# Attention's first step up to its exponentials, the second's scores and the third's mask tiles inside the last projection batch

## The reference

```
x = x + xattn(layernorm(x), ctx, ctx, mask, bias)     # x, ctx: (8, 512, 512)
x = x + ffn(layernorm(x))

def xattn(Q, K, V, mask, bias):
    q, k, v = heads(Q @ Wq.T + bq), heads(K @ Wk.T + bk), heads(V @ Wv.T + bv)
    scores = einsum('bhqd,bhkd->bhqk', q, k) / sqrt(32)
    scores = where(mask == 0, -1e9, scores) + bias    # bias: (1, 16, 512, 512)
    return merge(softmax(scores) @ v) @ Wo.T + bo
```

## Time and profile before

| what | value |
|---|---|
| median of three runs | 1814.23 us |
| the profiled execution | 1813.97 us, span 1812.1 us |
| TensorE, VectorE, ScalarE, GpSimd busy | 99%, 57%, 45%, 46% of the span |
| project | 0 to about 291 us |
| attend | about 291 to 861 us |
| blend | the rest |

### The profile page before, as it was taken

One profiled execution on the slowest core, in us unless ns is written; L12 is line 12 of the kernel. 1 busy time (PEld: TensorE's weight loads), 2 busy tenths in 40 slices (PEclk: granted clock), 3 DMA queues, 4 the chain that ended last, 5 costly groups with the idle time before them and its releaser, 6 DMA issues.

```text
span 1812.1 us, 29631 instructions
## 1 busy us (share of the span) xinstructions
PE 1786.0 (99%) x10784; PEld 1335.4 (74%) x10784; DVE 1039.6 (57%) x2431; ACT 815.5 (45%) x1814; POOL 833.0 (46%) x371
## 2 busy tenths in 40 slices
PE   8999998999999999999999999999999999999999
PEld 6888885555555555555778888888888888888887
DVE  6565556999999999998842334224332242342411
ACT  4222224999999999998232212113131131311300
POOL 1211127999999999997221231222312322223211
PEclk9999998999999999999999999999999999999999
DMA  8998999445436426330543554535546355464453
GB/s 292 339 359 315 324 335 376 144 140 192 136 121 207 140 95 233 105 119 19 200 131 117 199 179 162 203 123 191 180 140 231 123 187 174 138 210 163 150 187 128
DMA packets 198142, 339.97 MB, mean 188 GB/s; under 512 B 10608, under 2 KB 52208, under 8 KB 197488
## 3 DMA queue, kind: packets, MB, share of 16 engines
q1 hardware_dynamic: 194736, 325.50, 53.1%
q0 software_dynamic: 3264, 12.58, 1.9%
HBM read 268.84 MB, written 69.21 MB: 187 GB/s over the span
## 4 chain that ended last, share of the span: by engine, by line
PE 50%; DVE 1%; ACT 0%; issue 0%; POOL 0%; DVEq 0%
PE n_ps_y L1572 19%; PE n_ps_h L1551 19%; PE n_ps_m L1475 9%; PE n_ps_y L1475 3%; PE n_ps_m L1469 1%; DVE k_x L1318 0%; DVE h_bias L1237 0%; DVE k_x L1173 0%; PE n_ps_y L1469 0%; PE n_ps_h L1524 0%; PE n_ps_h L1527 0%; DVE h_k L1246 0%; DVE n_stats L1176 0%; POOL n_g_l L1145 0%; ACT L1431 0%
## 5 line engine op out<-in xcount | busy, mean ns | idle before, releaser
L1145 POOL TENSOR_TENSOR n_g_l<-h_pos,n_g_h 128x512 fp32r<-128x512 f32 x128 | 175.2, 1369 | 602.8 <-DVE n_g_h L1326 602.8
L1551 PE MATMUL n_ps_h<-n_zT_h,n_w 128*128 128x512 f32 x1024 | 336.7, 390 | 1.4 <-ACT h_pos L1431 1.4
L1572 PE MATMUL n_ps_y<-n_w,n_g_h 128*128 128x512 f32 x1024 | 316.6, 390 | 0.3 <-POOL n_g_l L1145 0.3
L1431 ACT ACTIVATE h_pos<-n_ps_h 128x512 f32<-128x512 f32 x128 | 75.8, 599 | 512.4 <-PE n_ps_h L1551 512.3
L1326 DVE CAST n_g_h<-h_pos 128x512 fp32r<-128x512 f32 x128 | 55.3, 434 | 379.5 <-ACT h_pos L1431 379.5
L1551 PEld LDWEIGHTS n_ps_h<-n_zT_h,n_w 128*128 128x128 f32 x1024 | 192.3, 188 | 41.5 <-issue 1.8
L1572 PEld LDWEIGHTS n_ps_y<-n_w,n_g_h 128*128 128x128 f32 x1024 | 191.2, 188 | 39.7 <-POOL n_g_l L1145 0.7
L1572 PE MATMUL n_ps_y<-n_w,n_g_l 128*128 128x512 f32 x512 | 199.3, 389 | 0.0
L1551 PE MATMUL n_ps_h<-n_zT_l,n_w 128*128 128x512 f32 x512 | 199.2, 389 | 0.0
L932 ACT ACTIVATE l_tiles<-l_tiles,a_nmax 128x512 f32<-128x512 f32 x256 | 182.6, 717 | 13.9 <-DVE a_nmax L873 13.9
L932 ACT ACTIVATE a_t_s<-a_t_s,a_nmax 128x512 f32<-128x512 f32 x256 | 182.8, 718 | 0.0
(11 more groups left out here) (198 smaller groups left out, 3158.2 us busy)
## 6 DMA issues: line engine op xcount, KB each, us to landing
n_w<-wf_d SPq DMA_DIRECT2D x256, 512.0 KB, 4.2
a_pos<-pos_d SPq DMA_DIRECT2D x24, 1024.0 KB, 5.6
l_tiles<-in_x SPq DMA_DIRECT2D x8, 1024.0 KB, 10.1
l_bias<-in_mask SPq DMA_DIRECT2D x8, 1024.0 KB, 14.4
k_d<-p_k_s SPq DMA_DIRECT2D x8, 1024.0 KB, 12.1
pos_d<-p_pos SPq DMA_DIRECT2D x8, 1024.0 KB, 13.4
v_d<-p_v_s SPq DMA_DIRECT2D x32, 256.0 KB, 6.6
wf_d<-p_wf_h SPq DMA_DIRECT2D x16, 512.0 KB, 5.8
```

The source lines that it names most:

```text
L1145: pool.tensor_tensor(out=g_l[:, f % NG, :], in0=g_f[:, f % NG, :], in1=g_h[:, f % NG, :].bitcast(F32), op=ALU.subtract).then_inc(g_low, 1)
L1551: last = pe.matmul(ps_h[:, f % 2, :], stationary, moving, start=i == 0, stop=i == len(passes) - 1)
L1572: last = pe.matmul(ps_y[:, t, :], gs[i], w2[:, f % NW, j, :], start=f == 0 and m == 0, stop=f == NF - 1 and m == 2)
```

## The change

`Late` gets a third pair of buffers, the semaphores of attention's scores, minima and exponentials, the small table of minima and sums, and the four PSUM banks that project used for turning x and attend for its scores. `k_s` and `pos` of project now lie in the third pair. In the last projection batch:

- TensorE makes the four scores of step 0 between the first and the second Q product, and the scores of step 1 after the last Q product;
- VectorE makes the four minima of step 0 between its first and second eviction of Q;
- ScalarE makes the four exponentials of step 0 after its last copy of feed-forward weights;
- GpSimd makes the mask tiles of step 2 in one instruction after its last difference of feed-forward weights;
- SP loads the bias rows of step 3 before it stores V. These rows lie where `pos` was, so SP first waits until the store of `pos` has landed.

Attend leaves these parts out. Nothing that is computed changes.

```diff
@@ class Late
-        self.tiles = [sb("tiles0"), sb("tiles1")]
-        self.bias = [sb("bias1"), sb("bias2")]
+        self.tiles = [sb("tiles0"), sb("tiles1"), sb("tiles2")]
+        self.bias = [sb("bias1"), sb("bias2"), sb("bias3")]
...
@@ project
-        x_raw, xn = late.tiles
-        c_raw, m_raw = late.bias
+        x_raw, xn, k_s = late.tiles
+        c_raw, m_raw, pos = late.bias
...
                 sp.wait_ge(bank_free, NPB + NVQ * b + NT)
+                if not more:
+                    sp.wait_ge(pos_out, 16 * (B + 1))
+                    load_bias(3)
                 for c in range(NC):
                     sp.dma_start(tokens(v_d[B * c + b]), v_s[:, :, c * P:(c + 1) * P]).then_inc(v_out, 16)
...
+            def third_mask_tiles():
+                pool.wait_ge(ahead.bias_in[2], 16)
+                pool.wait_ge(k_out, 16 * (B + 1))
+                pool.tensor_tensor(out=late.tiles[2][:, :, :], in0=ahead.pos[:, 2:3, :].broadcast_to([P, HG, S]),
+                                   in1=late.bias[1][:, :, :], op=ALU.subtract).then_inc(ahead.nbm_pool, HG)
...
+            def first_minima():
+                for i in range(HG):
+                    dve.wait_ge(late.scored, i + 1)
+                    dve.wait_ge(ahead.nbm_pool, HG)
+                    gate(dve, passed)
+                    dve.tensor_tensor_reduce(late.tiles[0][:, i:i + 1, :], late.ps[:, i:i + 1, :],
+                                             late.tiles[0][:, i:i + 1, :], 1.0, 3.0e38, ALU.add, ALU.min,
+                                             late.nmax[:, 0, i:i + 1]).then_inc(late.summed, 1)
...
+                if not more:
+                    for i in range(HG):
+                        act.wait_ge(late.summed, i + 1)
+                        act.activation(late.tiles[0][:, i, :], late.tiles[0][:, i, :], ACT.Exp, scale=-1.0,
+                                       bias=late.nmax[:, 0, i:i + 1], accum_out=late.total[:, 0, 0, i:i + 1]) \
+                            .then_inc(late.exped, 1)
...
                 for c in range(NC):
                     product(Q_AT + c, features((w_h[0], w_l[0]), (xT_h, xT_l), c))
+                    if not more and c == 0:
+                        pe.wait_ge(ahead.qk_in[0], 32)
+                        pe.wait_ge(fac_row_done, B)
+                        scores(0)
+                if not more:
+                    pe.wait_ge(late.summed, HG)
+                    scores(1)
@@ attend
-            sp.dma_start(bias_rows(0, HG, 3), bias[0, 0:HG, 3 * P:4 * P, :].rearrange("h p n -> p h n")) \
-                .then_inc(ahead.bias_in[3], 16)
...
-                        if g or j > 1:
+                        if g or j > 2:
                             step(hg, g, j, half)
...
-                    for i in range(HG):
+                    for i in range(HG if g or j > 1 else 0):
```

More of the change, by code:

```diff
@@ L86, in __init__, with sb @@
     def __init__(self, nc, stack):
-        def sb(name):
-            return stack.enter_context(nc.sbuf_tensor("l_" + name, [P, HG, S], F32, side="right"))
-        self.tiles = [sb("tiles0"), sb("tiles1")]
-        self.bias = [sb("bias1"), sb("bias2")]
+        def sb(name, shape=(P, HG, S)):
+            return stack.enter_context(nc.sbuf_tensor("l_" + name, list(shape), F32, side="right"))
+        self.tiles = [sb("tiles0"), sb("tiles1"), sb("tiles2")]
+        self.bias = [sb("bias1"), sb("bias2"), sb("bias3")]
+        self.small = sb("small", (P, 8 * HG))
+        self.nmax = self.small[:, 0:4 * HG].rearrange("p (n h) -> p n h", h=HG)
+        self.total = self.small[:, 4 * HG:8 * HG].rearrange("p (a b h) -> p a b h", a=2, b=2)
+        self.ps = stack.enter_context(nc.psum_tensor("l_ps", [P, HG, S], F32))
+        self.scored, self.summed, self.exped = (
+            stack.enter_context(nc.semaphore("l_" + n)) for n in ("scored", "summed", "exped"))
 class Kept:
@@ L163, in project @@
         cT_h, cT_l = sb("cT_h", [P, NC, S], F32R), sb("cT_l", [P, NC, S], F32R)
-        k_s = sb("k_s", [P, NC, S])
         v_s = sb("v_s", [P, NT, D])
-        pos = sb("pos", [P, NT, S])
         pos_min = sb("pos_min", [P, NT])
@@ L174, in project @@
         wf = sb("wf", [P, 2, 2, D])
-        stats = sb("stats", [P, NT, 6])
-        mv = sb("mv", [P, NT, 2])
+        stats = late.small[:, 0:NT * 6].rearrange("p (t n) -> p t n", t=NT)
+        mv = late.small[:, NT * 6:NT * 8].rearrange("p (t n) -> p t n", t=NT)
         var_e = sb("var_e", [P, NT])
         rstd = sb("rstd", [P, NT])
-        ps_t = ctx.enter_context(nc.psum_tensor("p_ps_t", [P, NC, S], F32))
+        ps_t = late.ps
         ps_j = ctx.enter_context(nc.psum_tensor("p_ps_j", [P, NPB, D], F32))
@@ L384, in body @@
                                    op=ALU.subtract).then_inc(wf_low, 1)
+                if not more:
+                    third_mask_tiles()
             walk(pool, body)
@@ L460, in body @@
                         .then_inc(bank_free, 1)
+                    if not more and c == 0:
+                        first_minima()
             for c in range(NC):
@@ L520, in _, with scores @@
             pe.wait_ge(consts_made, 3)
+            def scores(qt):
+                for i in range(HG):
+                    rows = slice(i * DK, (i + 1) * DK)
+                    pe.matmul(late.ps[:, i, :], ahead.q[rows, 0, qt * P:(qt + 1) * P], ahead.k[rows, 0, :],
+                              start=True, stop=True).then_inc(late.scored, 1)
             def body(b, more):
@@ L593, in attend @@
         pos_more = sb("pos", [P, NG - 1, NT, S])
-        bias_rows_of = [ahead.bias, *late.bias, sb("bias3", [P, HG, S])]
-        t_s = [*late.tiles, sb("t_s2", [P, HG, S]), sb("t_s3", [P, HG, S])]
-        nmax = sb("nmax", [P, NN, HG])
+        bias_rows_of = [ahead.bias, *late.bias]
+        t_s = [*late.tiles, sb("t_s3", [P, HG, S])]
+        nmax, total = late.nmax, late.total
         pT = sb("pT", [P, 2, HG, NT, HALF])
-        total = sb("total", [P, 2, 2, HG])
         rinv = sb("rinv", [P, 2, 2, HG, 1])
@@ L601, in attend @@
         r_rows = sb("r_rows", [P, 2, HALF])
-        ps_s = ctx.enter_context(nc.psum_tensor("a_ps_s", [P, HG, S], F32))
+        ps_s = late.ps
         ps_t = ctx.enter_context(nc.psum_tensor("a_ps_t", [P, 3, S], F32))
@@ L611, in attend @@
         nbm_pool, nbm_dve = ahead.nbm_pool, sem("nbm_dve")
-        scored, summed, exped, turned = sem("scored"), sem("summed"), sem("exped"), sem("turned")
+        scored, summed, exped, turned = late.scored, late.summed, late.exped, sem("turned")
         kept_act, kept_dve, weighed = sem("kept_act"), sem("kept_dve"), sem("weighed")
@@ L778, in step @@
                         pe.wait_ge(qk_in[b], 32 * g + 32)
-                    if at := lagged(g, j, 1):
+                    if g == 0 and j < 2:
+                        pass
+                    elif at := lagged(g, j, 1):
                         pe.wait_ge(summed, tiles(at) + HG)
@@ L882, in step @@
             def step(g, j, more):
-                if more:
+                if more and (g or j):
                     for i in range(HG):
```

## The result

The changed kernel takes 1809.08 us, median of nine runs (1808.38 to 1810.54), beside 1813.47 for the kernel before in nine runs: ratio 0.9978, 95% interval 0.9969 to 0.9986. That is 4.4 us, a gain that is there but lies within the 0.3% that the forecast took as the bound. Profiled, it is 1808.38 (span 1806.5) against 1813.97 (span 1812.1), 5.6 us less.

What follows compares the result with a forecast made beforehand. Bound: the ring of scores and minima, 4.39 us a step, not yet turning at the seam. Step 4 comes earlier by the smaller of 6.3 (ring) and 5.8 (`pos` landing), so 1813.97 becomes 1808.2; range 1805 to 1812.5.

Steps and rivals of the forecast that it cites:

- the 0.3% that the forecast took as the bound: Whole run: about 0.3%, 5.4 us, is what a measurement of this kernel can tell from no change.
- The parts in project: Last projection batch: scores 1.14 each, second Q eviction 0.3 late, third mask tiles done 2.7 us before attend; these cost nothing.
- V's stores: SP in the last projection batch: they start at 281.8, take 2.8 us and end at 284.6.
- The row of batch 4: Nearest earlier case: mask landed 4.8 us after V's stores began, and they took 2.75; basis for forecasting 2.8.
- They end at 284.6 ... now to 290.2 at the latest: SP behind V's stores: Q and weight stores take 5.56 as before, ending 0.9 before the last Q eviction.
- The sum: Minima of step 4: from 311.60 to 305.8, 5.8 us earlier, the smaller of 6.3 and 5.8.
- The rival of a queue held midway: SP in project: V's stores held up by 1.9 more, gain 4.4, 1809.6; chance 0.10.
- The same bytes stand ahead of that load as before, so I expect 301.2: Load of `pos` of batch 1 in attend: issued at 293.0, lands at 301.2 again, 300.9 at best.
- The ring: Attend, scores and minima waiting on each other: steps 1 to 4 take three times 4.28, or 13.18; step 4 5.9 to 6.3 earlier.
- GpSimd alone binds: Step 4 of attend: GpSimd's tiles wait for `pos`, take 4.55, end at 305.75; minima start at 305.8.
- The clock: Start of attend: stays at full through 300; rival falls over two steps, 2.9 less 0.5, gain 3.4, 1810.6; chance 0.13.
- Evictions held by GpSimd: Q evictions in project wait for GpSimd's mask tiles: attend 3.1 later, gain 3.2, 1810.8; chance 0.03.

Runs made afterwards that it cites:

- no_third: Changed kernel with the third mask tiles and their bias rows back in attend: 1808.51 us, ratio 0.9981 to the kernel before.
- early1_after: Changed kernel with the bias rows of step 1 loaded one projection batch earlier: 1806.72 us, ratio 0.9958 to the kernel before.
- cut_bias: no_third with only one of four heads of step 3's bias rows loaded, so step 3 is not attention's: 1807.82 us, ratio 0.9965.
- v_behind: Changed kernel with `pos` of batches 1 to 3 loaded ahead of V of batches 1 to 3: 1809.08 us, ratio 0.9980.
- bias_last: Changed kernel with the bias rows of step 3 loaded behind Q's last store instead of ahead of V's stores: 1808.74 us, ratio 0.9979.
- before_filled_both: Kernel before with ten unread matmuls behind the last Q product and 22 unread turns between scores of steps 0 and 1: 1811.20 us, ratio 0.9986.
- early1_last: bias_last with the bias rows of step 1 loaded one projection batch earlier: 1808.43 us, ratio 0.9969 to the kernel before.
- bias_last_pos_first: bias_last with `pos` of batch 1 as attend's first load: 1808.68 us, ratio 0.9984 to the kernel before.
- pos1_early2: early2 with `pos` of batch 1 loaded in project, where Wk's high part lay, which moves: 1811.61 us, ratio 1.0000.
- early2: early1_after with Q and K of batches 2 and 3 loaded in projection batch 4 instead of the last: 1806.86 us, ratio 0.9970.
- two filled forms: Kernel before with ten unread matmuls behind the last Q product (1812.88 us, ratio 1.0004), and that plus 22 unread turns (1811.20 us, 0.9986).

## Why the prediction was nearly right

- **The parts in project** hold. The scores take 1.14 each. The second Q eviction waits 0.24, for its product; the forecast had it 0.3 late behind the minima, which were done before. Neither costs anything. The third mask tiles end 4.7 us before GpSimd is wanted. That they, with their load, gain nothing at step 4 is shown by no_third.
- **V's stores** hold: forecast start 281.8, in the same frame 280.64 + 0.86 = 281.5; forecast length 2.8, measured 2.84. The row of batch 4 was the right one to take.
- **"They end at 284.6 ... now to 290.2 at the latest"** is the step that failed. SP's stores ended 12.42 after Q0 instead of the forecast 10.63, and attend began at 13.08, not 11.33. The sum carried the 5.56 of the stores behind V's over from before. But the first store of Q alone now held SP for 2.71 us, where it was 1.32; in no_third it was 1.66, in early1_after 2.38:

```profile
283.53 2.71 SPq L326 DMA_DIRECT2D q_d<-p_q_s  x1
282.93 1.66 SPq L323 DMA_DIRECT2D q_d<-p_q_s  x1
281.82 2.38 SPq L326 DMA_DIRECT2D q_d<-p_q_s  x1
```

  (The changed kernel, no_third, early1_after.) In the six kernels with the load ahead of V's stores it took 2.38 to 2.96, in the eight without 0.69 to 1.72. This alone does not delay attend: early1_after has it and begins at 11.45, because its V stores began 1.82 before Q0 and the long store was over before the second eviction. In the changed kernel they began 0.43 after Q0, since SP waited until the store of `pos` had landed, at Q0. no_third, with neither wait nor load, begins at 11.47. So the wait and the fuller queue together cost 1.6 us, put at nothing in the sum; the wait alone was not run. The rival of a queue held midway had a like price, 1.9, but looked for it in V's stores, and it came one store later.
- **"The same bytes stand ahead of that load as before, so I expect 301.2"** failed in its reason. The landing was at 301.15, in the frame of before 302.0, 0.8 late. Fewer bytes ahead (cut_bias) or no V behind (v_behind) did not bring it forward. In early1_after it was issued 1.67 earlier and landed 1.37 earlier, but the issue alone does not set it either: the kernel before issued it at 11.21 and it landed at 20.1, later than the 19.6 of early1_after, which issued it at 11.87. Over all kernels that load it in attend it was issued 11.2 to 13.6 after Q0 and landed at 19.6 to 21.0. What sets the landing was not found.
- **The ring** was nearly right: 12.84 (three times 4.28) or 13.18 was allowed for steps 1 to 4, read from before, where part of it ran at the half clock. With the full clock the changed kernel took 12.69, and without waits it would be 3.93 + 3.93 + 4.6 = 12.5.
- **The tie.** Scores of step 4 end at 305.83, GpSimd's tiles at 305.88. Forecast was that GpSimd alone binds. In fact both do, which is why bias_last, no_third and cut_bias, which start attend earlier and leave GpSimd's tiles where they were, gain at most 0.25 at step 4.
- **The clock** stayed at full as forecast, and its weight was looked at only as a rival. How large it is depends on the order of counting. The kernel before gains 2.05 when its fall is taken away (before_filled_both), and the changed kernel lies another 2.63 ahead of that. But in v_behind, the changed kernel with another order of loads, the clock fell, and step 4 came at 26.32, still 4.21 ahead of the kernel before. From the start of attend to step 4 the four changed kernels whose clock fell there (v_behind, early1_last, bias_last_pos_first, pos1_early2) took 13.7 to 14.0, the changed one 12.77. So a fall would have cost the changed kernel 0.9 to 1.2 us at step 4, an estimate, and left a gain of about 3.5 to 3.7. The rival had 2.4 less than the forecast, for a fall over two steps; in the traces the fall was over by the minima of step 2. So 2.05 in one order is about 1 in the other, and the clock's share and the overlap's can't be told apart by one subtraction. The sum itself needed no term for the clock, being made from start to start.
- **Evictions held by GpSimd**: no. Those at 280.21, 284.17 and 286.88 took 0.75 beside GpSimd's 279.60 to 288.77, while L461, four elements a row, again took 4.04 us from 271.41, beside GpSimd's 270.83 to 275.43; one batch before it took 0.17. By the rule of the Trainium skill, page "SBUF — State Buffer", section "Who interferes with whom", the minima too should go free; the trace agrees, 0.69 each.

The number: 5.8 us forecast, 4.68 measured at step 4 (1.1 less), plus 0.86 of scatter in this profile. So 1808.2 lies near the profiled 1808.38 partly by luck: step 4 won 1.1 less than forecast, and the scatter gave 0.86 back. Against the median, 1809.08, it is 0.9 low, and the medians lie 4.4 apart. The change stays under 0.3%, where the forecast leaned to just above it.

**What stays open:** why a clock fall comes in one kernel and not in another that stood as long (below), and whether the changed kernel falls in some of its runs. Its nine have a mean clock of 0.999 (1808.38 to 1809.08, four of them) or 0.998 (1808.86 to 1810.54), which would fit a fall in some; it was not shown. Open as well is what sets the landing of `pos`.

## What to carry to other kernels

Where work is pulled over a seam, follow the queue that ends the old stage store by store, and ask of each load put ahead of a store what later issue pays for it: one load of 1 MB, with the wait that it needed, cost 1.6 us behind V's stores. When the first wait is gone, list all that arrives within a microsecond of the next one; here three kernels with an earlier start gained nearly nothing at step 4, and moving a load into a batch with idle DMA time gained 2.0 us more in the median. And before crediting an overlap with its gain, fill the gap with work that nobody reads: it shows what the clock alone would have given. Then look at the changed kernel with a fall too, since the two gains need not add up.

## What was not expected of the hardware

- **The idle time ahead of a stretch does not tell whether the clock falls.** TensorE stood, ahead of attend's first work, 1.17 to 1.25 us in early2, early1_after, cut_bias and no_third, with no fall; 2.04 in bias_last (none) but 2.04 and 2.05 in early1_last and bias_last_pos_first (to 0.57 and 0.50); 2.38 in v_behind (0.50), 2.85 in the changed kernel (none), 2.87 in pos1_early2 (0.50). A fall of this sort costs 1.2 to 1.5 us up to the minima of step 2: from those of step 1 it takes 5.1 to 5.4 instead of 3.93. From the start of attend to step 4 it is 13.7 to 14.0 instead of 12.8.
- **K's matmuls ran slower once Wk's high part lay elsewhere in SBUF.** In pos1_early2 it shares the tile `l_pos` with `pos` of batch 1, at the other end. TensorE by form, 255 to 283 us, first in it, then in the changed kernel:

```profile
L580 PE MATMUL p_ps_j<-p_cT_h,l_pos 128*128 128x512 f32 x16 | 6.4, 398 | 0.0
L580 PE MATMUL p_ps_j<-p_cT_h,p_wk_l 128*128 128x512 f32 x16 | 6.4, 397 | 0.0
```

```profile
L572 PE MATMUL p_ps_j<-p_cT_h,p_wk_l 128*128 128x512 f32 x14 | 5.5, 390 | 0.0
L572 PE MATMUL p_ps_j<-p_cT_h,p_wk_h 128*128 128x512 f32 x13 | 5.1, 389 | 0.0
```

  397 ns against 389, and from start to start 0.233 against 0.227 us. The batches before the last follow each other at 35.00 us where early2, which did the same work, has 34.67, and the first Q eviction of the last one came at 282.84, 2.3 later. V's and Q's low forms kept their 389 to 390. Which property of the place does this, or whether the low part's new place has a share in it, was not tested.
- **The load of `pos`, 1 MB, took 7.3 to 8.9 us** at the start of attend, whatever stood ahead or behind. The bias rows of step 3, of the same size, took 5.0 to 5.6 as the first load of attend (the kernel before, its two filled forms, no_third) and 6.0 ahead of V's stores in the changed kernel.
